# A one-core recommender tower: seventeen tables by one-hot, the Gram in 64x64 tiles ahead of the MLP, one-hots in halves

## The chip, the cores and the metric

The kernel runs on one core of one Trainium2 chip. The metric is the device time of one execution in microseconds (us); several runs of the same program are summed up by their median. The core has five engines with instruction queues of their own that meet only at semaphores: TensorE (PE, products; its weight loads are listed as PEld), VectorE (DVE), ScalarE (ACT), GpSimd (POOL) and SyncE (SP, which here only issues transfers).

## The reference

For each of 2048 samples, 32 categorical fields pick one row of 64 numbers each out of 32 tables. Of the tables 13 have 12500 rows, 2 have 125000, 8 have 1250 and 9 have 1000. The 32 rows of a sample are multiplied with each other (a 32x32 Gram matrix), the 496 entries above the diagonal and 16 dense inputs are the 512 inputs of a small network.

```python
e = jnp.stack([tbl_0[ids[:, 0]], ..., tbl_31[ids[:, 31]]], axis=1)    # 2048 x 32 x 64
gram = jnp.einsum('bnd,bmd->bnm', e, e)
z = gram[:, rows, cols]                                               # rows, cols: above the diagonal, 496
h = jnp.concatenate([z, dense_ctx], axis=1)                           # 2048 x 512
h = jnp.maximum(h @ W_top1 + b_top1, 0.0)                             # 512
h = jnp.maximum(h @ W_top2 + b_top2, 0.0)                             # 256
y = h @ W_top3                                                        # 2048 x 1
```

All of it is float32.

## The kernel before

**Supers and steps.** The batch is cut into 8 supers of 256 samples (two tiles of 128, `TILES`). Step `s` of the program turns super `s` into pairs of products, finishes the network of super `s - 1` and looks up rows of super `s + 1`. Steps 1 to 6 are a loop of three passes with two steps each; step 0 and step 7 stand outside it.

**Two ways to fetch a row.** The 16 smallest tables (`LOOKED_UP`, called units) are held in SBUF, each float32 split into three bfloat16 parts (`split_sb`). DVE compares the ids with the row numbers (`make_onehot`, L495) into a 0/1 tile `onehot` of 125 partitions x 8 or 10 columns x 256 samples, one instruction a unit; PE multiplies it with the parts (`look_up`, L303, 16 or 20 products a unit) and DVE adds the three parts into `rows` (`add_parts`, L503). A ring of four one-hots lets DVE run three units ahead. The other 16 fields are gathered by POOL: 32 indirect DMAs a super (L253), each followed by a write of zeros into a tile nobody reads (`pause`, L260), 256 of each in all. POOL does nothing else until the end, and it waits for no engine unless it comes two supers ahead.

**A step on PE.** Eight groups of four fields are transposed into `emb_t` (L289); from the second on, one unit of the next super goes before each. Groups 4 to 7 wait for the gathers. Then come eight Gram batches (L316) of 8 products each. A product takes four samples (64 rows x 128 columns, against 128 columns) and so holds the 32x32 blocks of each sample against all four, of which the four on the diagonal are wanted; samples of the first tile lie on partitions 0 to 63, those of the second on 64 to 127. The profile lists a float32 product as two records. Ahead of batches 0 to 4 stand two units each (one in the fifth), ahead of batches 4 and 5 the halves of layer 1 of the super before (L328), ahead of 6 layer 2 (L338), ahead of 7 layer 3 (L345).

**After a batch.** ACT copies one half of the Gram columns to `folded` (L441), then DVE lays the other half over it by a mask (L530); PE may start batch `k` once DVE is through with batch `k - 2`. When all eight are folded, 16 DMAs of 32 KB (L192) carry the wanted blocks from `folded` to `pairs`, and four more put the dense inputs beside them; ten of the 16 are issued by SP and six by POOL in the last step, all by SP before. ACT waits for them before the first copy of the next step, since there is one `folded`.

**Start and end.** Until the first transpose, PE, DVE and ACT split the tables and look up super 0. The last step has no units to look up: it transposes with four banks, and PE issues products on the identity (L352) to stay busy, 32 before the last group of gathers and 10 behind it.

The program as it stood, with the line numbers of the profile:

## Time and profile before

| what | value |
|---|---|
| runs, us | 494.22, 495.32, 491.78; median 494.22 |
| profiled execution, us | 495.87 |
| its span (first to last instruction), us | 493.6 |
| mean granted TensorE clock | 0.959 |
| busy us: PE, DVE, ACT, POOL | 432.1, 302.9, 114.2, 407.9 |
| instructions in the profile | 10400 |

Busy time is the time in which an engine had at least one instruction under way. Records of PE overlap, so that a mean duration of a record there is much longer than the distance from one to the next. What an engine waits for stands in brackets behind a row of the timeline; "issue" means that nothing in the profile released it at that moment. Lines such as L316 are lines of the kernel above.

### The profile page before, as it was taken

The numbers are of one execution on the slowest core, as the hardware profiler recorded it, in microseconds if no ns is written. First come the engines' busy times: TensorE is split into PE (matmuls) and PEld (weight loads), VectorE is DVE, ScalarE is ACT, GpSimd is POOL, SyncE is SP. The second block draws the span as 40 slices with busy tenths as digits, with TensorE's granted clock in tenths as the row PEclk, the third lists the DMA queues.
The fourth block names the chain that finished last, engine by engine and source line by source line (L and its number), as shares of the span: only waits on it lengthen the run. The fifth ranks groups of instructions, "written<-read, shape, count | busy, mean of one in ns | idle before, by whom it ended". The sixth has DMA issues, their size and how long they took to land.

```text
span 493.6 us, 10400 instructions
## 1 busy us (share of the span) xinstructions
PE 432.1 (88%) x4200; PEld 387.7 (79%) x4200; DVE 302.9 (61%) x369; ACT 114.2 (23%) x206; POOL 407.9 (83%) x522
## 2 busy tenths in 40 slices
PE   5298889989799989978999699988999679984987
PEld 5287789989598889877988599777988679874765
DVE  2499969968672698267925586366935847340400
ACT  2244313122012221231123110321113201230322
POOL 7999889999998899999988999889988999884110
PEclk9699999999999999999999899988999979995999
DMA  4534751012311222112311231122211231121010
GB/s 109 144 139 150 215 136 31 16 20 62 87 37 23 47 60 80 21 44 57 86 23 32 54 101 20 23 54 71 62 23 31 51 106 17 23 43 34 7 39 1
DMA packets 21814, 29.32 MB, mean 59 GB/s; under 512 B 9782, under 2 KB 14070, under 8 KB 20640
## 3 DMA queue, kind: packets, MB, share of 16 engines
q1 hardware_dynamic: 12980, 18.96, 11.3%
q0 software_dynamic: 8384, 8.60, 11.2%
q10 hardware_dynamic: 404, 1.09, 0.6%
q8 instruction: 37, 0.61, 0.5%
q14 instruction: 9, 0.07, 0.0%
HBM read 24.35 MB, written 0.07 MB: 49 GB/s over the span
## 4 chain that ended last, share of the span: by engine, by line
POOL 82%; issue 9%; PE 4%; DMA 2%; SPq 1%; DVE 1%; ACT 1%; DVEq 0%
POOL rows L253 59%; POOL pause L260 22%; PE mlp_ps L328 1%; PE gram_ps L316 1%; SPq L192 1%; PE mlp_ps L338 1%; DVE folded L530 1%; DMA rows<-tbl,index 0%; ACT folded L441 0%; PE gram_ps L352 0%; SPq L219 0%; DMA pairs<-dense 0%; DMA pairs<-folded 0%; DMA index<-ids 0%; PE turn_ps L289 0%
## 5 line engine op out<-in xcount | busy, mean ns | idle before, releaser
L253 POOL DMA_INDIRECT rows<-tbl,index x256 | 293.8, 1148 | 44.5 <-issue 42.1
L303 PE MATMUL turn_ps<-split_sb,onehot 125*128 125x192 bf16 x2272 | 213.5, 251 | 22.9 <-DVE split_sb L544 11.7
L303 PEld LDWEIGHTS turn_ps<-split_sb,onehot 125*128 125x128 bf16 x2272 | 193.7, 100 | 33.7 <-DVE split_sb L544 15.5
L495 DVE TENSOR_TENSOR onehot<-place,codes_wide 125x2048 bf16<-125x2048 f16 (+1 forms) x131 | 174.2, 1331 | 7.1 <-DMA place<-ids_scratch 7.1
L260 POOL MEMSET pause<- 128x384 f32 x256 | 111.5, 436 | 0.2
L503 DVE TENSOR_REDUCE rows<-turn_ps 128x128 f32<-128x384 f32 x128 | 71.1, 556 | 54.0 <-PE turn_ps L303 31.1
L530 DVE COPY_PREDICATED folded<-second_sb,gram_ps 128x512 f32<-128x512 int32 x64 | 46.7, 730 | 82.9 <-issue 47.7
L316 PE MATMUL gram_ps<-emb_t 64*128 64x128 f32 x1024 | 76.4, 288 | 3.7 <-DVE folded L530 2.2
L316 PEld LDWEIGHTS gram_ps<-emb_t 64*128 64x128 f32 x1024 | 63.8, 191 | 19.1 <-issue 14.8
L441 ACT COPY folded<-gram_ps 128x512 f32<-128x512 f32 x64 | 37.6, 587 | 150.4 <-PE gram_ps L316 132.3
L328 PE MATMUL mlp_ps<-pairs,w_sb 128*128 128x256 f32 x256 | 58.5, 383 | 1.2 <-DMA pairs<-dense 1.2
L404 ACT COPY emb_t<-mlp_ps 128x512 f32<-128x512 f32 x58 | 34.1, 588 | 101.2 <-PE mlp_ps L289 63.9
L289 PE MATMUL mlp_ps<-ident_sb,rows 128*128 128x128 f32 x240 | 38.8, 284 | 17.9 <-DMA rows<-tbl,index 11.3
L328 PEld LDWEIGHTS mlp_ps<-pairs,w_sb 128*128 128x128 f32 x256 | 47.5, 190 | 8.4 <-DMA pairs<-dense 1.7
L289 PEld LDWEIGHTS mlp_ps<-ident_sb,rows 128*128 128x128 f32 x240 | 27.5, 145 | 20.5 <-issue 19.0
L352 PE MATMUL gram_ps<-ident_sb 128*128 128x128 f32 x232 | 33.1, 301 | 4.5 <-DMA ident_sb<-identity 4.5
L352 PEld LDWEIGHTS gram_ps<-ident_sb 128*128 128x128 f32 x232 | 30.1, 158 | 4.5 <-DMA ident_sb<-identity 4.5
L338 PE MATMUL mlp_ps<-h,w_sb 128*128 128x256 f32 x128 | 29.6, 384 | 0.0
L421 ACT ACTIVATE h<-mlp_ps,b_sb 128x256 f32<-128x256 f32 x32 | 13.5, 472 | 58.7 <-PE mlp_ps L328 46.3
L338 PEld LDWEIGHTS mlp_ps<-h,w_sb 128*128 128x128 f32 x128 | 23.7, 190 | 3.8
L486 DVE COPY y<-mlp_ps 1x256 f32 (+1 forms) x8 | 5.0, 620 | 23.4 <-PE mlp_ps L345 23.4
L192 POOL DMA_DIRECT2D pairs<-folded x6 | 3.0, 513 | 17.6 <-DVE folded L530 17.6
(28 smaller groups left out, 75.7 us busy)
## 6 DMA issues: line engine op xcount, KB each, us to landing
place<-ids_scratch SPq DMA_DIRECT2D x8, 1000.0 KB
rows<-tbl,index POOLq DMA_INDIRECT x256
pairs<-folded SPq DMA_DIRECT2D x122, 32.0 KB
emb_t<-tbl SPq DMA_DIRECT2D x8, 250.0 KB
folded<-tbl SPq DMA_DIRECT2D x5, 312.5 KB
w_sb<-w SPq DMA_DIRECT2D x1, 1024.0 KB
place<-ids_scratch ACTq DMA_DIRECT2D x1, 750.0 KB
rows<-tbl SPq DMA_DIRECT2D x2, 312.5 KB
```

What stands on the lines that cost most here:

```text
L253: nc.gpsimd.indirect_dma_start(rows[:, s % 2, slot, t, :], None, tables[f][:, :], bass.IndirectOffsetOnAxis(index[:, s, t, f:f + 1], 0),). ...
L260: nc.gpsimd.memset(pause[:], 0.0).then_inc(paused, 1)
L289: last = nc.tensor.transpose(turn_bank[g % banks][:, k, :], rows[:, parity, GROUP_F * g + k].rearrange("p t d -> p (t d)"), ident_sb[:])
L303: last = nc.tensor.matmul(turn_ps[:, u % 2].rearrange("p k b -> p (k b)")[:, t * PARTS * DIM:(t + 1) * PARTS * DIM], onehot[:, u % RING, c ...
L316: last = nc.tensor.matmul(gram_ps[:, k % 2, t, u // TILES].rearrange("p h ij -> p (h ij)"), e.rearrange("p b f -> p (b f)"), e.rearrange(" ...
L328: last = nc.tensor.matmul(mlp_ps[:, o // 2, o % 2, :], w1_sb[:, jj, P * o:P * (o + 1)], pairs[:, parity, :, jj, :], start=(jj == 0), stop= ...
L338: last = nc.tensor.matmul(mlp_ps[:, 0, o, :], w2_sb[:, k, P * o:P * (o + 1)], h1[:, k, :], start=(k == 0), stop=(k == OT1 - 1))
L352: nc.tensor.transpose(gram_ps[:, 0, 0].rearrange("p u h ij -> p (u h ij)")[:, 0:P], ident_sb[:], ident_sb[:])
L441: nc.scalar.copy(folded[:, :, :, BATCH_Q * k:BATCH_Q * (k + 1)].rearrange("p i j (q t) -> p (i j) q t", t=TILES), gram_ps[:, k % 2, :, :, ...
L495: nc.vector.tensor_tensor(onehot[:, u % RING, 0:SPAN[u], :], place[:, parity, u, :].unsqueeze(1).to_broadcast([TP, SPAN[u], SUPER]), codes ...
L503: nc.vector.reduce_sum(rows[:, parity, u, :, :], turn_ps[:, u % 2].rearrange("p k b -> p (k b)")[:, 0:TILES * PARTS * DIM] .rearrange("p ( ...
L530: nc.vector.copy_predicated(folded[:, :, :, BATCH_Q * k:BATCH_Q * (k + 1)].rearrange("p i j (q t) -> p (i j) q t", t=TILES), second_sb[:]. ...
```

## The change

There are four edits.

1. `UNITS` goes from 16 to 17: the last table with 1250 rows is looked up as well, and POOL gathers 15 fields, 30 DMAs a super.
2. A Gram product takes two samples in place of four (64 rows x 64 columns, against 64 columns), and writes to partitions 0 to 63 or 64 to 127 of `gram_ps`. There are 128 products a super in place of 64, in four batches of 32, and a quarter of the columns each. `folded` has half the columns for a sample, two copies by parity, and ACT no longer waits for the moves.
3. The eight slots of the second half of a step remain, but only the first four have a Gram batch; the halves of layer 1, layer 2 and layer 3 stay ahead of slots 4 to 7.
4. `make_onehot` issues two instructions of half the columns.

PE in the loop's first step, from the fourth Gram batch on, before (`gram_ps` is the Gram's PSUM tile, `turn_ps` that of the units, `mlp_ps` that of the layers):

```order
L316 MATMUL gram_ps<-emb_t 128x128 [waits second_copied]
L316 MATMUL gram_ps<-emb_t 128x128 x7
L300 REGISTER_ALU [waits looked_up]
L303 MATMUL turn_ps<-split_sb,onehot 128x192 [waits onehot_ready]
L303 MATMUL turn_ps<-split_sb,onehot 128x192 x19
L324 REGISTER_ALU
L328 MATMUL mlp_ps<-pairs,w_sb 128x256 [waits dense_placed_even]
L328 MATMUL mlp_ps<-pairs,w_sb 128x256 x7
L311 REGISTER_ALU
L316 MATMUL gram_ps<-emb_t 128x128 [waits second_copied]
L316 MATMUL gram_ps<-emb_t 128x128 x7
L328 MATMUL mlp_ps<-pairs,w_sb 128x256 [waits y_ready]
```

And the same place now:

```order
L323 MATMUL gram_ps<-emb_t 64x64 [waits second_copied]
L323 MATMUL gram_ps<-emb_t 64x64 x31
L305 REGISTER_ALU [waits looked_up]
L308 MATMUL turn_ps<-split_sb,onehot 128x192 [waits onehot_ready]
L308 MATMUL turn_ps<-split_sb,onehot 128x192 x19
L305 REGISTER_ALU [waits looked_up]
L308 MATMUL turn_ps<-split_sb,onehot 128x192 [waits onehot_ready]
L308 MATMUL turn_ps<-split_sb,onehot 128x192 x19
L331 REGISTER_ALU
L335 MATMUL mlp_ps<-pairs,w_sb 128x256 [waits dense_placed_even]
L335 MATMUL mlp_ps<-pairs,w_sb 128x256 x7
L335 MATMUL mlp_ps<-pairs,w_sb 128x256 [waits y_ready]
```

The fourth batch is now the last, two units stand behind it in place of one, and the halves of layer 1 follow each other with no batch between them.

DVE in the same step, one Gram slot, before:

```order
L530 COPY_PREDICATED folded<-second_sb,gram_ps 128x64x8 [waits first_copied]
L502 REGISTER_ALU
L503 TENSOR_REDUCE rows<-turn_ps 128x128 [waits lookup_ready]
L495 TENSOR_TENSOR onehot<-place,codes_wide 125x2560
L502 REGISTER_ALU
L503 TENSOR_REDUCE rows<-turn_ps 128x128 [waits lookup_ready]
L495 TENSOR_TENSOR onehot<-place,codes_wide 125x2560
```

Now:

```order
L504 COPY_PREDICATED folded<-second_sb,gram_ps 128x32x16 [waits first_copied]
L525 REGISTER_ALU
L526 TENSOR_REDUCE rows<-turn_ps 128x128 [waits lookup_ready]
L518 TENSOR_TENSOR onehot<-place,codes_wide 125x1280 x2
L525 REGISTER_ALU
L526 TENSOR_REDUCE rows<-turn_ps 128x128 [waits lookup_ready]
L518 TENSOR_TENSOR onehot<-place,codes_wide 125x1280 x2
```

Each one-hot is two instructions now, and the fold has as many elements as before but of twice as many samples.

```diff
--- before.py
+++ after.py
...
-BATCH_Q = 8
+SIDE = 2
+SLOTS = 8
+BATCH_Q = 16
+GRAM_IN_SLOT = range(GRAM_BATCHES)
...
-LOOKED_UP = sorted(range(FIELDS), key=lambda f: (VOCAB[f], f))[:16]
+LOOKED_UP = sorted(range(FIELDS), key=lambda f: (VOCAB[f], f))[:17]
-FIRST_UNITS = 16
+FIRST_UNITS = 17
...
-GRAM_UNITS = [[7, 8], [9, 10], [11, 12], [13, 14], [15]]
+GRAM_UNITS = [[7, 8], [9, 10], [11, 12], [13, 14], [15, 16]]
-GRAM_UNITS += [[]] * (GRAM_BATCHES - len(GRAM_UNITS))
+GRAM_UNITS += [[]] * (SLOTS - len(GRAM_UNITS))
...
-    return rows, np.tile(second, (QUAD, QUAD))
+    return rows, np.tile(second, (QUAD, SIDE))
 def build(nc, ids, tables, dense, w1, b1, w2, b2, w3, identity, second, looked_ids, codes, out):
...
-        folded = sb("folded", [P, QUAD, HALF, QUADS], fp32)
+        folded = sb("folded", [P, 2, SIDE, HALF, QUADS], fp32)
...
-        second_sb = sb("second_sb", [P, QUAD * HALF], i32)
+        second_sb = sb("second_sb", [P, SIDE * HALF], i32)
...
-        spare = [(8, emb_t[0:TP].rearrange("p b f -> p (b f)")), (6, folded[0:TP].rearrange("p i j q -> p (i j q)")),
+        spare = [(8, emb_t[0:TP].rearrange("p b f -> p (b f)")), (6, folded[0:TP].rearrange("p h i j q -> p (h i j q)")),
...
-        gram_ps = ps("gram_ps", [P, 2, TILES, BATCH_Q // TILES, 2, QUAD * HALF], fp32)
+        gram_ps = ps("gram_ps", [P, 2, TILES, BATCH_Q // TILES, 2, SIDE * HALF], fp32)
...
         def move_cells(engine, i, jq, parity):
-                                    folded[FIELDS * i:FIELDS * (i + 1), i, CHUNKS * jq:CHUNKS * (jq + 1), :])
+                                    folded[FIELDS * i:FIELDS * (i + 1), parity, i % SIDE, CHUNKS * jq:CHUNKS * (jq + 1), :])
         def _(sp):
...
             def gram_batch(s, k):
-                for u in range(BATCH_Q):
-                    quad = BATCH_Q * k + u
-                    t, q = u % TILES, (BATCH_Q * k + u) // TILES
-                    e = emb_t[DIM * t:DIM * (t + 1), QUAD * q:QUAD * (q + 1), :]
-                    last = nc.tensor.matmul(gram_ps[:, k % 2, t, u // TILES].rearrange("p h ij -> p (h ij)"),
-                                            e.rearrange("p b f -> p (b f)"),
-                                            e.rearrange("p b (h j) -> p h b j", h=2),
-                                            start=True, stop=True)
+                for u in range(BATCH_Q // TILES):
+                    for i in range(0, QUAD, SIDE):
+                        for t in range(TILES):
+                            b = QUAD * (BATCH_Q // TILES * k + u) + i
+                            e = emb_t[DIM * t:DIM * (t + 1), b:b + SIDE, :]
+                            last = nc.tensor.matmul(
+                                gram_ps[FIELDS * i:FIELDS * (i + SIDE), k % 2, t, u].rearrange("p h ij -> p (h ij)"),
+                                e.rearrange("p b f -> p (b f)"), e.rearrange("p b (h j) -> p h b j", h=2),
+                                start=True, stop=True)
             def layer1_tile(s, o, parity, turn):
...
-                for k in range(GRAM_BATCHES):
+                for k in range(SLOTS):
...
-                    gram_batch(s, k)
+                    if k in GRAM_IN_SLOT:
+                        gram_batch(s, k)
...
+            def copy_first(s, k, parity):
+                act.wait_ge(gram_ready, GRAM_BATCHES * s + k + 1)
+                nc.scalar.copy(
+                    folded[:, parity, :, :, BATCH_Q * k:BATCH_Q * (k + 1)].rearrange("p i j (q t) -> p (i j) q t", t=TILES),
+                    gram_ps[:, k % 2, :, :, 0, :].rearrange("p t q ij -> p ij q t")).then_inc(first_copied, 1)
             def layer2_drain(s):
...
             def step(s, parity, mlp=True, ahead=True):
-                for k in range(GRAM_BATCHES):
+                for k in range(SLOTS):
-                    if k == 0 and (mlp or not ahead):
-                        act.wait_ge(pairs_moved, 16 * len(MOVES) * s)
-                    act.wait_ge(gram_ready, GRAM_BATCHES * s + k + 1)
-                    nc.scalar.copy(folded[:, :, :, BATCH_Q * k:BATCH_Q * (k + 1)].rearrange("p i j (q t) -> p (i j) q t", t=TILES),
-                                   gram_ps[:, k % 2, :, :, 0, :].rearrange("p t q ij -> p ij q t")).then_inc(first_copied, 1)
+                    if k in GRAM_IN_SLOT:
+                        copy_first(s, k, parity)
             def high(u):
...
+            def fold_second(s, k, parity):
+                dve.wait_ge(first_copied, GRAM_BATCHES * s + k + 1)
+                dve.sem_inc(folds_begun, 1)
+                nc.vector.copy_predicated(
+                    folded[:, parity, :, :, BATCH_Q * k:BATCH_Q * (k + 1)].rearrange("p i j (q t) -> p (i j) q t", t=TILES),
+                    second_sb[:].unsqueeze(2).unsqueeze(2).to_broadcast([P, SIDE * HALF, BATCH_Q // TILES, TILES]),
+                    gram_ps[:, k % 2, :, :, 1, :].rearrange("p t q ij -> p ij q t")).then_inc(second_copied, 1)
             def make_onehot(s, u, parity, first=False, loads=None):
-                nc.vector.tensor_tensor(onehot[:, u % RING, 0:SPAN[u], :],
-                                        place[:, parity, u, :].unsqueeze(1).to_broadcast([TP, SPAN[u], SUPER]),
-                                        codes_wide[:, CODE_AT[SPAN[u]]:CODE_AT[SPAN[u]] + SPAN[u], :],
-                                        ALU.is_equal).then_inc(onehot_ready, 1)
+                half = SPAN[u] // 2
+                for c in (0, half):
+                    code = CODE_AT[SPAN[u]] + c
+                    last = nc.vector.tensor_tensor(onehot[:, u % RING, c:c + half, :],
+                                                   place[:, parity, u, :].unsqueeze(1).to_broadcast([TP, half, SUPER]),
+                                                   codes_wide[:, code:code + half, :], ALU.is_equal)
+                last.then_inc(onehot_ready, 1)
             def add_parts(s, u, parity, first=False):
...
-                for k in range(GRAM_BATCHES):
+                for k in range(SLOTS):
-                        if k >= GRAM_BATCHES - READY_MADE:
-                            make_onehot(s + 2, k - (GRAM_BATCHES - READY_MADE), parity, loads=loads)
+                        if k >= SLOTS - READY_MADE:
+                            make_onehot(s + 2, k - (SLOTS - READY_MADE), parity, loads=loads)
-                    dve.wait_ge(first_copied, GRAM_BATCHES * s + k + 1)
-                    dve.sem_inc(folds_begun, 1)
-                    nc.vector.copy_predicated(
-                        folded[:, :, :, BATCH_Q * k:BATCH_Q * (k + 1)].rearrange("p i j (q t) -> p (i j) q t", t=TILES),
-                        second_sb[:].unsqueeze(2).unsqueeze(2).to_broadcast([P, QUAD * HALF, BATCH_Q // TILES, TILES]),
-                        gram_ps[:, k % 2, :, :, 1, :].rearrange("p t q ij -> p ij q t")).then_inc(second_copied, 1)
+                    if k in GRAM_IN_SLOT:
+                        fold_second(s, k, parity)
             def take_high(u):
```

The tables, ids and biases that the host lays out follow from `UNITS` and from `slot_meaning` by themselves.

## Rows read from the trace of the kernel before

**Rows 1.** The page, part 1: busy us of each engine, its share of the span, instructions.

```profile
PE 432.1 (88%) x4200; PEld 387.7 (79%) x4200; DVE 302.9 (61%) x369; ACT 114.2 (23%) x206; POOL 407.9 (83%) x522
```

**Rows 2.** The page, part 4: the chain that ended last, its shares of the span by line.

```profile
POOL rows L253 59%; POOL pause L260 22%; PE mlp_ps L328 1%; PE gram_ps L316 1%; SPq L192 1%; PE mlp_ps L338 1%; DVE folded L530 1%; DMA rows<-tbl,index 0%; ACT folded L441 0%; PE gram_ps L352 0%; SPq L219 0%; DMA pairs<-dense 0%; DMA pairs<-folded 0%; DMA index<-ids 0%; PE turn_ps L289 0%
```

**Rows 3.** Groups by form: line, engine, op, out<-in, shapes, count; busy us, mean ns; idle before.

```profile
L253 POOL DMA_INDIRECT rows<-tbl,index x256 | 293.8, 1148 | 44.5 <-issue 42.1 <-DMA index<-ids 2.4
...
L260 POOL MEMSET pause<- 128x384 f32 x256 | 111.5, 436 | 0.2
...
L495 DVE TENSOR_TENSOR onehot<-place,codes_wide 125x2048 bf16<-125x2048 f16 x75 | 91.0, 1215 | 7.1 <-DMA place<-ids_scratch 7.1
...
L495 DVE TENSOR_TENSOR onehot<-place,codes_wide 125x2560 bf16<-125x2560 f16 x56 | 83.3, 1487 | 0.0
...
L316 PE MATMUL gram_ps<-emb_t 64*128 64x128 f32 x1024 | 76.4, 288 | 3.7 <-DVE folded L530 2.2 <-issue 0.9 <-DVE rows L503 0.3
```

**Rows 4.** Instructions on tile rows, the gather alone: duration ns minimum/median/maximum.

```profile
L253 POOL DMA_INDIRECT rows<-tbl,index x256: 952/953/2427, 2.9 to 448.4; - x128
```

**Rows 5.** Timeline of POOL and DVE, 19 to 23 us: start us, duration us, engine, line.

```profile
19.27 1.23 DVE L495 TENSOR_TENSOR onehot<-place,codes_wide 125x2048 bf16<-125x2048 f16 x1 [7.13 <-DMA place<-ids_scratch]
...
20.09 1.23 POOL L253 DMA_INDIRECT rows<-tbl,index  x1 [0.17 <-issue]
...
20.41 0.68 DVE L539 TENSOR_TENSOR pairs<-emb_t,split_sb 125x512 f32<-125x512 f32 x1
...
21.61 1.22 DVE L495 TENSOR_TENSOR onehot<-place,codes_wide 125x2048 bf16<-125x2048 f16 x1
...
21.91 1.74 POOL L253 DMA_INDIRECT rows<-tbl,index  x1 [0.17 <-issue]
...
22.75 0.69 DVE L539 TENSOR_TENSOR h<-emb_t,split_sb 125x512 f32<-125x512 f32 x1
```

**Rows 6.** Timeline of PE while the small tables are split, to the first transpose.

```profile
60.12 1.81 PE L303 MATMUL turn_ps<-split_sb,onehot 125*128 125x192 bf16 x20 [0.43 <-issue]
...
63.46 1.81 PE L303 MATMUL turn_ps<-split_sb,onehot 125*128 125x192 bf16 x20 [0.43 <-issue]
...
71.41 0.66 PE L289 MATMUL mlp_ps<-ident_sb,rows 128*128 128x128 f32 x4 [0.65 <-DVE rows L503]
```

**Rows 7.** Timeline of PE, steps 0 to 4: first transposes, one Gram batch, one landing wait.

```profile
109.50 0.66 PE L289 MATMUL mlp_ps<-ident_sb,rows 128*128 128x128 f32 x4
...
184.92 1.16 PE L316 MATMUL gram_ps<-emb_t 64*128 64x128 f32 x16
...
186.02 3.47 PE L303 MATMUL turn_ps<-split_sb,onehot 125*128 125x192 bf16 x40
...
215.51 0.65 PE L289 MATMUL mlp_ps<-ident_sb,rows 128*128 128x128 f32 x4 [2.57 <-issue]
...
230.03 0.65 PE L289 MATMUL mlp_ps<-ident_sb,rows 128*128 128x128 f32 x4 [1.98 <-DMA rows<-tbl,index]
...
265.81 0.66 PE L289 MATMUL mlp_ps<-ident_sb,rows 128*128 128x128 f32 x4
```

**Rows 8.** Timeline of PE and POOL, the last step and the end.

```profile
435.47 0.66 PE L289 MATMUL mlp_ps<-ident_sb,rows 128*128 128x128 f32 x4
...
439.37 3.66 PE L352 MATMUL gram_ps<-ident_sb 128*128 128x128 f32 x32
...
448.39 0.95 POOL L253 DMA_INDIRECT rows<-tbl,index  x1 [0.17 <-issue]
...
450.89 1.11 PE L289 MATMUL turn_ps<-ident_sb,rows 128*128 128x128 f32 x4 [7.86 <-DMA rows<-tbl,index]
...
460.49 2.42 PE L316 MATMUL gram_ps<-emb_t 64*128 64x128 f32 x32 [0.30 <-DVE folded L530]
...
463.21 2.42 PE L316 MATMUL gram_ps<-emb_t 64*128 64x128 f32 x32 [0.30 <-DVE folded L530]
...
490.11 1.02 PE L345 MATMUL mlp_ps<-h,w_sb 128*1 128x256 f32 x4 [0.56 <-ACT h L427]
```

5 lines of the change are left out of this document (4 added, 1 removed).

## The prediction

> **What bounds the kernel now.** I read the chain of waits first. Four fifths of it are POOL: 59% gathers and 22% pauses [rows 2]. PE is busy for a larger share of the span, 88% [rows 1], so the second question is how much room PE has. It shows where the last group of transposes stands: PE waited 1.98 us for a landing in step 3 and 7.86 us in the last step [rows 7, 8]. POOL leads and PE follows a few per cent behind; both have to get shorter for the kernel to gain much.
>
> **POOL, its price list.** A gather takes 0.953 us when nothing meets it [rows 4] and 1.148 in the mean, the pause 0.436, and 42.1 us of issue over 256 is 0.164 [rows 3]. So a gather with its pause costs 1.553 bare, and on top come 293.8 - 256 x 0.953 = 49.8 us over the execution, 0.195 a gather. The early timeline shows what they are [rows 5]. The gather of 20.09 met the one-hot that ran from 19.27 to 20.50 and took 1.23; the one of 21.91 met the one-hot from 21.61 to 22.83 and took 1.74. Both agree with one rule: about 0.12 us after its start the gather needs something that the one-hot holds, and it gets it when that instruction ends (20.50 - 20.21 = 0.29 against 0.28 too long; 22.83 - 22.03 = 0.80 against 0.79). In both cases another instruction of DVE with two SBUF inputs had started 0.09 and 0.08 us before that end (20.41, 22.75), and the gather did not wait for this one too. So POOL gets through between two instructions that follow each other closely.
>
> The Trainium skill, "SBUF — State Buffer", section "Who interferes with whom", says the same: a DVE instruction with two SBUF inputs contends with a GpSimd instruction that reads SBUF, and the loser is blocked until the instruction ends. It would make nothing of the sum different.
>
> **Edit 4, halves.** One-hots cost 1.215 us for 2048 elements and 1.487 for 2560 [rows 3], so 0.531 ns an element and 0.127 fixed; a half is 0.671 or 0.807. What a gather that comes at a random moment waits is the sum of the squared durations over twice the period. Before: (9 x 1.215² + 7 x 1.487²)/2 = 14.4 over 32 x 1.748 = 55.9 us gives 0.258; measured are 0.195, or 0.76 of it, since the two engines are not independent. After: 9 x 0.671² + 8 x 0.807² = 9.3 over some 50.5 us gives 0.184, times 0.76 gives **0.14**. The ends: 0, and 0.22 if two halves hold POOL out like one instruction (0.195 x 17/16, over a period a tenth shorter). I take 0.14, since the rows at 20.41 and 22.75 are exactly this case.
>
> **Edit 1 on POOL.** 240 gathers in place of 256. The last one starts at 2.9 + 239 x (1.553 + 0.14) = 407.5; before it was 448.39 [rows 8]. That is 41 us earlier, of which 28 are the 16 gathers with their present price and 13 the shorter waits. Its rows land 2.5 later, at 410.
>
> **PE, its own pace.** First the start: the last units before the first transpose follow each other every 3.34 us (60.12 to 63.46) [rows 6], so a 17th unit costs that, and two instructions in place of one cost DVE 0.04 each time, as consecutive ones overlap by 0.09 and the fixed part is 0.127: 0.7 in all. Step 0 begins at 71.41 + 4.0 = 75.5.
>
> A step that waits for nothing takes 265.81 - 215.51 - 1.98 = 48.3 us, and the way back of the loop 2.57, once in two steps: 49.6 [rows 7]. Step 0 took 109.50 - 71.41 = 38.1, steps 1 and 2 together 215.51 - 109.50 = 106.0 [rows 6, 7]. A Gram batch costs 186.02 - 184.92 = 1.10, eight of them 8.8 a step. Unit 17 adds half of the 3.40 that 40 records of units take: 1.7 [rows 7]. Where no batch covers ACT, PE waits ahead of layer 3, 0.56 in the last row [rows 8]: 0.6 a step. So each of steps 1 to 6 loses 8.8 - 1.7 - 0.6 = 6.5, step 0 loses 7.1, and each gains G, the four new batches.
>
> **Edit 2, G.** The trace has no 64x64 tile; this is the term I know least. What it has: 16 records of 64x128 take 1.10 us, while a record's mean duration is 0.288 [rows 3, 7], so the two halves of the array do run side by side. A keep-warm product of the full array takes 3.66/32 = 0.114 [rows 8]. So a half takes as long for a record as the full array, and 16 in pairs take 8 x 0.112 = 0.9, plus 0.2 for draining at the change.
> - Low end: four tiles side by side, half the columns each. 64 records are 16 rounds of 0.056, with 0.2 behind: 1.1 a batch, G = 4.4.
> - Middle: only row halves overlap, column halves take turns: 32 rounds, 2.0 a batch, G = 8.0.
> - High end: a record costs 0.056 whatever its width, by its issue: 64 x 0.056 + 0.2 = 3.8, G = 15.1.
>
> I take 4.4, since the row halves overlap fully and two records of a pair cost no more than one.
>
> The Trainium skill, "TensorEngine Tiling (Array Packing)", section "Instruction Overhead", speaks against it: each matmul has some 60 cycles of overhead, so that a smaller one doesn't get cheaper. By its figure, an estimate of 25 ns for each of 64 records, a batch would be 1.8 us, G 7.2 and the time some 467. The trace shows no record that small.
>
> **The sum.** PE is through with step 6 at 75.5 + (38.1 - 7.1) + (106.0 + 4 x 49.6 - 6 x 6.5) + 7 G = 371.9 + 7 G, and stands ready for the last group 7.6 later (435.47 to 439.37 + 3.66) [rows 8]: 379.5 + 7 G, with G = 4.4 at **410.3**. POOL's rows are there at **410**. A tie, so each will at times wait for the other; I add 1.5 and let the last group start at 411.5, where it started at 450.89: 39.4 earlier.
>
> Behind it, two pairs of batches fall away, each 463.21 - 460.49 = 2.72 [rows 8], since a drain of the same size now serves 16 quads: 5.4 earlier. The moves, dense inputs and the two networks at the end stay. Span 493.6 - 39.4 - 5.4 = 448.8. The profiled execution was 2.3 longer than its span and 1.65 over the median of the runs, so I forecast 448.8 + 2.3 - 1.7 = **449.5**.
>
> **Costed at nothing**, with the cover named. DVE's work in a Gram slot, one fold, two sums and two one-hots, grows by 0.08 us; PE's slot was 1.1 + 3.4 us with no wait for DVE ahead of its batch [rows 7] and keeps that length. How much room DVE had there I can't read from these rows: if the halves bound it, three slots a step would grow by 0.1 each, 2 us in all. ACT's waiting for moves goes, but moves start four slots earlier now and layer 1 needs them a step later. `folded` at twice the copies moves the same bytes. The index of supers 1 to 7 is loaded behind 17 tables in place of 16, and POOL asks for it only at 2.9 + 30 x 1.7 = 54 us. The first three one-hots of the super after next are made in slots 5 to 7, while PE is in the layers. The layer-3 copy has one unit on PE to hide behind.
>
> **Rivals.**
> - *Column halves take turns* (chance 0.14). PE leads from G = 4.4 on. Before, the last batch ended at 463.21 + 2.42 = 465.6 [rows 8]; now it would end at the time at which PE is ready, plus 14 products of 0.114 (four transposes, ten to keep busy), plus G. With 8.0 that is 435.5 + 1.6 + 8.0 = 445.1, 20.5 earlier, or **474**. For it: no row shows a column tile. Against: the row halves.
> - *A floor per record* (0.10), whatever the tiles do: anything above 17 ns a record makes a batch longer than the 1.3 us at which PE clearly leads. At half the present 0.056 a batch is 2.0 us and the time again 474. For it: a quarter of the work in twice the instructions. Against: nothing in the present 0.056 needs one. The Trainium skill's page on tiling, cited above, is this rival's only source of a figure.
> - *Halves hold POOL out like a whole one-hot* (0.06). Then 0.22 a gather: the last start is at 2.9 + 239 x 1.773 = 426.6, 21.8 earlier, and with 5.4 behind it the time is **467**. Against it stand the rows at 20.41 and 22.75.
> - *PE's issue bounds and the kernel gets slower* (0.06). Twice the products, each at the old price of a record, in the Gram batches. The last batch ends at 379.5 + 7 G + 1.6 + G, which meets the 465.6 of before at G = 10.6, or (2.65 - 0.2)/64 = 38 ns a record. At the high end, 15.1, it ends at 501.9 and the time is **530**. Against it: two records and their loads now pass in 112 ns, and their width explains that.
> - *In between, G from 10 to 11* (0.03): within 1% of before.
> - *Fewer waits than I count* (0.04): with no waits of gathers POOL is done by 377, and PE sooner than my sum by some 4 us, as steps 1 and 2 (106.0 in place of 2 x 48.3 + 2.6) hold stalls that needn't come back: about 444.
>
> The rest, 0.57, is the forecast, from 443 to 458 by its bounds. The range takes in the first three rivals: 442 to 475. About 1% is what a measurement can tell from no change here. Faster by more than that 0.90, same 0.03, slower 0.07.
>
> **What would show it.** The gather's mean: 1.09 us if halves work, 1.17 if not. A Gram batch from its first product to the next unit: 1.1, 2.0 or 3.8 us for 64 records. The last group's wait for landed rows: near zero in a tie, some us if POOL still leads, none and a POOL that ends early if PE does; the chain of waits then is PE's. The start of the first transpose at 75.5. Gram batches at the end every 1.4 us. Wrong would be the whole reading if DVE's sums or one-hots released PE in the Gram slots.

## The result, and the profile after

| | before | after |
|---|---|---|
| median of the runs beside each other, us | 493.0 (4 runs) | 477.06 (475.72 to 479.38, 4 runs) |
| profiled execution, its span, us | 495.87, 493.6 | 479.38, 477.6 |
| granted clock | 0.959 | 0.939 |
| gathers: count, mean ns | 256, 1148 | 240, 1215 |
| start of the last gather, us | 448.39 | 437.38 |
| last group of transposes, us | 450.89 | 439.86 |

The ratio is 0.968 (95%: 0.962 to 0.974). The kernel got faster, but by 16 us and not by 44: the forecast was 449.5, the range ended at 475. Little more than a third of the expected gain arrived.

The chain of waits of the changed kernel, shares of the span by line, against [rows 2]:

```profile
POOL 83%; issue 9%; PE 4%; DMA 2%; SPq 2%; DVE 0%; ACT 0%; DVEq 0%
POOL rows L258 61%; POOL pause L265 22%; PE mlp_ps L335 2%; SPq L197 1%; PE gram_ps L323 1%; PE mlp_ps L345 1%; DMA rows<-tbl,index 1%; PE gram_ps L359 0%; DMA pairs<-dense 0%; SPq L224 0%; DMA pairs<-folded 0%; DMA index<-ids 0%; DVE folded L504 0%; ACT folded L434 0%; PE turn_ps L294 0%
```

POOL leads as before. The groups of POOL and of the Gram (line, engine, out<-in, count; busy us, mean ns; idle before), against [rows 3]:

```profile
L258 POOL DMA_INDIRECT rows<-tbl,index x240 | 291.6, 1215 | 41.8 <-issue 39.4
...
L265 POOL MEMSET pause<- 128x384 f32 x240 | 105.4, 439 | 0.1
...
L323 PE MATMUL gram_ps<-emb_t 64*64 64x64 f32 x2048 | 37.8, 223 | 0.7 <-DVE folded L504 0.7
```

Sixteen gathers fewer cost POOL almost as much busy time as before (293.8). The timeline of PE shows the rest: the first transpose, one batch, the first waits for rows, the way back of the loop, the last step and the end (start us, duration us):

```profile
75.34 0.66 PE L294 MATMUL mlp_ps<-ident_sb,rows 128*128 128x128 f32 x4 [0.65 <-DVE rows L526]
...
132.49 1.11 PE L294 MATMUL mlp_ps<-ident_sb,rows 128*128 128x128 f32 x4 [8.88 <-DMA rows<-tbl,index]
...
183.65 1.16 PE L323 MATMUL gram_ps<-emb_t 64*64 64x64 f32 x64
184.74 1.99 PE L308 MATMUL turn_ps<-split_sb,onehot 125*128 125x192 bf16 x22
...
217.30 0.68 PE L294 MATMUL mlp_ps<-ident_sb,rows 128*128 128x128 f32 x2 [3.62 <-issue]
222.51 0.58 PE L294 MATMUL mlp_ps<-ident_sb,rows 128*128 128x128 f32 x2 [4.52 <-issue]
...
424.74 0.66 PE L294 MATMUL mlp_ps<-ident_sb,rows 128*128 128x128 f32 x4
...
439.86 1.11 PE L294 MATMUL turn_ps<-ident_sb,rows 128*128 128x128 f32 x4 [7.89 <-DMA rows<-tbl,index]
...
474.06 1.02 PE L352 MATMUL mlp_ps<-h,w_sb 128*1 128x256 f32 x4 [0.56 <-ACT h L441]
```

The first transpose and the batch (184.74 - 183.65 = 1.09) are as forecast. What isn't: in step 1 PE waits 8.88 us for gathered rows, and in the last step 7.89.

**Where POOL's time went.** This is the start, POOL and then DVE:

```profile
43.80 0.43 POOL L265 MEMSET pause<- 128x384 f32 x1
44.39 2.81 POOL L258 DMA_INDIRECT rows<-tbl,index  x1 [0.17 <-issue]
47.20 0.43 POOL L265 MEMSET pause<- 128x384 f32 x1
```

```profile
43.36 1.55 DVE L518 TENSOR_TENSOR onehot<-place,codes_wide 125x1280 bf16<-125x1280 f16 x2
44.83 0.82 DVE L558 TENSOR_TENSOR h<-folded,split_sb 125x640 f32<-125x640 f32 x1
45.56 0.82 DVE L563 TENSOR_TENSOR split_sb<-pairs,split_sb 125x640 bf16<-125x640 f32 x1
46.30 0.55 DVE L526 TENSOR_REDUCE rows<-turn_ps 128x128 f32<-128x384 f32 x1
```

By the rule of [rows 5] the gather of 44.39 needs something at 44.51, meets the second half and gets it when that ends, at 44.91. It took 2.81 us; a free gather has 0.953 - 0.12 = 0.83 left from there, so it got it at 46.37, when the second subtraction ended (45.56 + 0.82 = 46.38). It was passed over at two boundaries between instructions with two SBUF inputs and got through only where the sum of parts, which reads PSUM, came next. The same in a Gram slot, and beside it a case that went well (gathers of POOL, then the one-hots on DVE that they met):

```profile
96.13 1.94 POOL L258 DMA_INDIRECT rows<-tbl,index  x1 [0.16 <-issue]
...
143.71 1.34 POOL L258 DMA_INDIRECT rows<-tbl,index  x1 [0.17 <-issue]
```

```profile
95.70 1.55 DVE L518 TENSOR_TENSOR onehot<-place,codes_wide 125x1280 bf16<-125x1280 f16 x2
...
143.41 1.55 DVE L518 TENSOR_TENSOR onehot<-place,codes_wide 125x1280 bf16<-125x1280 f16 x2
```

Each row is two halves of some 0.82, overlapping by 0.09. The gather of 143.71 got through at 143.71 + 1.34 - 0.83 = 144.22, the end of the first half (143.41 + 0.82). The one of 96.13 missed the end of the first (96.52) and got through at 97.24, the end of the second (97.25).

Counted over all gathers: above 240 x 0.953 they spend 63 us. 27 gathers were held past the end of the instruction that they met, 13 of them before the first transpose (17.1 us past it) and 14 later (10.2 us). These 27.3 us are nearly the whole distance from the forecast, which had 240 x 0.14 = 34 us of waits; without them the waits later are 0.139 a gather, where I had put 0.14. In the kernel before none was held so.

### The profile page after: what moved, and what is told of

It reads as the page before. It is cut to its first block, busy times and chain, and to the rows that moved or that the text cites. A ratio compares the mean times of both kernels' runs of the same rounds, so it can differ in the third digit from the quotient of the medians.

```text
span 477.6 us, 12826 instructions
## 1 busy us (share of the span) xinstructions
PE 407.4 (85%) x5394; PEld 373.2 (78%) x5394; DVE 307.2 (64%) x494; ACT 97.2 (20%) x176; POOL 399.6 (84%) x490
## 3 DMA queue, kind: packets, MB, share of 16 engines
q1 hardware_dynamic: 13110, 19.78, 12.4%
## 4 chain that ended last, share of the span: by engine, by line
POOL 83%; issue 9%; PE 4%; DMA 2%; SPq 2%; DVE 0%; ACT 0%; DVEq 0%
POOL rows L258 61%; POOL pause L265 22%; PE mlp_ps L335 2%; SPq L197 1%; PE gram_ps L323 1%; PE mlp_ps L345 1%; DMA rows<-tbl,index 1%; PE gram_ps L359 0%; DMA pairs<-dense 0%; SPq L224 0%; DMA pairs<-folded 0%; DMA index<-ids 0%; DVE folded L504 0%; ACT folded L434 0%; PE turn_ps L294 0%
## 5 line engine op out<-in xcount | busy, mean ns | idle before, releaser
L258 POOL DMA_INDIRECT rows<-tbl,index x240 | 291.6, 1215 | 41.8 <-issue 39.4
L308 PE MATMUL turn_ps<-split_sb,onehot 125*128 125x192 bf16 x2432 | 227.1, 252 | 18.9 <-DVE split_sb L563 16.2
L308 PEld LDWEIGHTS turn_ps<-split_sb,onehot 125*128 125x128 bf16 x2432 | 208.5, 100 | 26.5 <-DVE split_sb L563 20.8
L518 DVE TENSOR_TENSOR onehot<-place,codes_wide 125x1024 bf16<-125x1024 f16 (+1 forms) x278 | 194.4, 746 | 6.5 <-DMA place<-ids_scratch 6.5
L526 DVE TENSOR_REDUCE rows<-turn_ps 128x128 f32<-128x384 f32 x136 | 75.3, 554 | 56.9 <-PE turn_ps L308 53.2
L265 POOL MEMSET pause<- 128x384 f32 x240 | 105.4, 439 | 0.1
L434 ACT COPY folded<-gram_ps 128x512 f32<-128x512 f32 x32 | 18.8, 586 | 128.6 <-PE gram_ps L323 128.6
L323 PE MATMUL gram_ps<-emb_t 64*64 64x64 f32 x2048 | 37.8, 223 | 0.7 <-DVE folded L504 0.7
L323 PEld LDWEIGHTS gram_ps<-emb_t 64*64 64x64 f32 x2048 | 33.6, 137 | 5.7 <-issue 5.6
L504 DVE COPY_PREDICATED folded<-second_sb,gram_ps 128x512 f32<-128x512 int32 x32 | 23.1, 721 | 11.5 <-ACT folded L434 11.5
```

The costliest lines, as they stand in the source:

```text
L258: nc.gpsimd.indirect_dma_start(rows[:, s % 2, slot, t, :], None, tables[f][:, :], bass.IndirectOffsetOnAxis(index[:, s, t, f:f + 1], 0),). ...
L265: nc.gpsimd.memset(pause[:], 0.0).then_inc(paused, 1)
L308: last = nc.tensor.matmul(turn_ps[:, u % 2].rearrange("p k b -> p (k b)")[:, t * PARTS * DIM:(t + 1) * PARTS * DIM], onehot[:, u % RING, c ...
L323: last = nc.tensor.matmul(gram_ps[FIELDS * i:FIELDS * (i + SIDE), k % 2, t, u].rearrange("p h ij -> p (h ij)"), e.rearrange("p b f -> p (b ...
L504: nc.vector.copy_predicated(folded[:, parity, :, :, BATCH_Q * k:BATCH_Q * (k + 1)].rearrange("p i j (q t) -> p (i j) q t", t=TILES), secon ...
L518: last = nc.vector.tensor_tensor(onehot[:, u % RING, c:c + half, :], place[:, parity, u, :].unsqueeze(1).to_broadcast([TP, half, SUPER]), ...
```

## The experiments

The ratios are to the kernel before on the same chip; its median was 493.0, 493.2, 493.1, 492.9 and 491.0 in the five jobs (groups of kernels that ran beside each other). Jobs 1 and 2 ran on one chip, job 3 on a second, jobs 4 and 5 on a third. "Held" are gathers kept past the end of the instruction that they met. Where an expectation uses letters, A is the theory that POOL's losses at the boundaries are the cause, B that halves are innocent of them, L that PE's loop jump is the cause, F that the refill of `place` is, and S that the long Gram batches belong to one job and not to the kernel.

| run | job | median, us | ratio (95%) | waits of gathers beyond 0.953, us | held: count, us |
|---|---|---|---|---|---|
| the change | | 477.06 | 0.968 (0.962 to 0.974) | 63 | 27: 27.3 |
| e3 gaps | 1 | 478.16 | 0.967 (0.960 to 0.973) | 34 | 0 |
| f1 gaps again | 4 | 452.33 | 0.917 (0.914 to 0.921) | 36 | 0 |
| f4 change, refill early | 4 | 477.99 | 0.970 (0.965 to 0.976) | 61 | 25: 25.3 |
| e8 change, refill of one row | 2 | 478.13 | 0.969 (0.965 to 0.974) | 62 | 23: 23.8 |
| e11 whole one-hots, refill early | 3 | 470.41 | 0.956 (0.953 to 0.958) | 55 | 0 |
| f3 whole at the start alone | 4 | 466.36 | 0.944 (0.939 to 0.949) | 50 | 17: 12.4 |
| e4 before, halves | 1 | 496.74 | 1.007 (1.003 to 1.010) | 49 | 19: 20.8 |
| g2 before, halves | 5 | 498.96 | 1.013 (1.006 to 1.021) | 54 | 18: 20.0 |
| g1 before, halves, gaps | 5 | 479.35 | 0.975 (0.969 to 0.981) | 34 | 0 |
| e12 fastest | 3 | 442.45 | 0.900 (0.896 to 0.903) | 51 | 0 |

**Gaps (e3, f1, f2).** The direct test: a one-column memset of 0.06 us on DVE between the two halves, and around the subtractions of the start, so that no two instructions with two SBUF inputs follow each other directly in DVE's program. The work stays the same.

```diff
+            def gap_one():
+                n = next(gaps)
+                nc.vector.memset(gap[:, n:n + 1], 0.0)
...
                 for c in (0, half):
+                    if c:
+                        gap_one()
...
+                gap_one()
                 low(u)
+                gap_one()
```

> The change with a DVE write of one column (128x1, no SBUF input) between the two halves of each one-hot, and at the start also between the subtractions that follow, so that no two instructions with two SBUF inputs follow each other. Theory A: no gather waits past the end of the instruction it met; excess about 7 at the start and 0.14 x 209 = 29 us behind it, 36 in place of 63; PE then sets the end as often as POOL, time 450 to 456. Theory B: the excess stays near 63, time 477 or slightly more for the added instructions.

POOL did just this: none held, its last gather at 408.7. The time did not move: 478.16, and the chain was PE's. I took that for a second cause, the refill of `place`, and two more runs seemed to bear it out (below). But its profile had long Gram batches that nothing explained, so the same kernel ran again:

> The kernel with the one-column memset between two halves, run a second time, because its Gram batches need explaining: in its first profile 22 of its 28 batches of 64 records between units took 1.2 to 2.2 us where the changed kernel's take 1.09 to 1.14, 16.2 us in all, and they were long already in step 0, ahead of the first transfer of place that the other kernels treat differently. Theory F (the refill of place costs PE 27 us): about 478 again, with the long batches. Theory S (the long batches are something of that job and not of the kernel; the refill costs PE only what is left, 27 - 13 = 14 us over six steps): batches of 1.1 us and 478 - 16 = 462, with POOL's last gather near 410 as before.

The same kernel took 452.33, less than either theory had. This is one Gram batch of step 0 in the first run, and then in the second (PE's timeline):

```profile
92.38 1.14 PE L325 MATMUL gram_ps<-emb_t 64*64 64x64 f32 x58
93.83 0.36 PE L325 MATMUL gram_ps<-emb_t 64*64 64x64 f32 x6 [0.31 <-issue]
94.13 3.47 PE L310 MATMUL turn_ps<-split_sb,onehot 125*128 125x192 bf16 x40
```

```profile
91.97 1.16 PE L325 MATMUL gram_ps<-emb_t 64*64 64x64 f32 x64
93.06 3.47 PE L310 MATMUL turn_ps<-split_sb,onehot 125*128 125x192 bf16 x40
```

In job 1, PE stopped inside its batches with nothing to wait for; they took up to 2.4 us in place of 1.1 in all three kernels with the new Gram (9, 20 and 22 of the 28 batches between units in e1, e2 and e3), and in none of any other job. What it was I can't say. It isn't the chip, since job 2 had the same one, and the long batches are only 16 of the 29 us that PE lost in e3 against f1 between its first transpose and its last step. The kernel before ran at 493.0 in that job; old batches aren't free of it either, since e4 has two long ones of 28 and the profile of the kernel before has one. So of job 1 (e1 to e4) only POOL's counts carry weight here, and its times are given without resting on them. The second run's POOL, PE's rows in its last step, and the chain by engine:

```profile
L260 POOL DMA_INDIRECT rows<-tbl,index x240 | 264.4, 1101 | 41.9 <-issue 39.4 <-DMA index<-ids 2.6
```

```profile
403.47 0.66 PE L296 MATMUL mlp_ps<-ident_sb,rows 128*128 128x128 f32 x4
...
407.04 3.66 PE L361 MATMUL gram_ps<-ident_sb 128*128 128x128 f32 x32
412.99 0.66 PE L296 MATMUL turn_ps<-ident_sb,rows 128*128 128x128 f32 x4 [2.29 <-DMA rows<-tbl,index]
```

```profile
POOL 82%; issue 9%; PE 4%; DMA 2%; SPq 2%; DVE 0%; ACT 0%; DVEq 0%
```

A gather 1.10 us, PE ready at 407.04 + 3.66 = 410.7, the last group at 413.0, span 449.8: nearly every number of the forecast (1.09, 410.3, 411.5, 448.8). In DVE's rows the memset costs next to nothing:

```profile
43.41 1.56 DVE L526 TENSOR_TENSOR onehot<-place,codes_wide 125x1280 bf16<-125x1280 f16 x2
44.18 0.06 DVE L513 MEMSET gap<- 128x1 f32 x1
```

The two halves take 1.56 us together where they took 1.55, and their records still overlap, by some 0.07 us. So what lets a gather through is the instruction between them and no idle time of DVE that the profile would show.

Could the memset have helped only by moving the gathers away from the bad boundaries? The distances say no. In the change, each of the 14 gathers held in the steps needed the port 0.55 to 0.56 us after the start of a first half of 0.82 us, as the one of 96.13 did (96.13 + 0.12 - 95.70 = 0.55); none of the 37 that got through at a boundary did so there, and the one of 143.71 had 0.42. Over the seven kernels whose halves touch (the change, e2, e4, e8, f3, f4, g2), 80 gathers met a first half of 0.82 us at 0.54 to 0.58 us and 72 of them were held, while all that met a half in the steps at another distance, or a half of 0.68 us, got through at its end. In the seven with the memset between halves (e3, e5, e6, e7, f1, f2, g1) 75 gathers met such a half at the same distance, and none was held.

**The refill of `place` (e5, f2, e6, e8, e7, f4).** SP refills `place`, 1.06 MB, behind the moves. These now begin four slots earlier, so that a refill begins beside each of PE's two loop jumps (205.3 and 303.3 us in f1). e5 and f2 are the gap kernel with the refill ahead of the moves (`refill_place(2 * pair + 4, ...)` ahead of `rearrange_pairs(2 * pair + 1, 1)`, and so on); e6 and e8 shrink it to one row, with gaps and without, and so leave out the ids: from super 2 on they look rows up by old ones.

```diff
-                sp.dma_start(place[:, parity], scratch.ap()[bass.ds(of, 1)].to_broadcast([TP, UNITS, SUPER])
+                sp.dma_start(place[0:1, parity, 0:1], scratch.ap()[bass.ds(of, 1), 0:1]
```

> As e3_gap, and SP issues the refill of the ids' broadcast tile (place, 1.06 MB) for the super after next ahead of a super's moves in place of behind them. In e3_gap PE set the end: its loop-backs (steps 2 to 3 and 4 to 5) took 9 to 11 us from the last product to the second group of transposes, less 1.8 in a step without a jump, and each time a refill had begun within 1 us of the jump, and an instruction fetch took 2.9 us in place of 1.0. Theory F (the refill starves PE's instruction fetch): the jumps fall to about 3 us each, the last step begins 8 to 12 us earlier, time 466 to 470. Theory L (the jump is longer since the loop body holds more instructions): no change, 478 within 3.

> As e3_gap, but a refill of place carries one row of one partition in place of 1.06 MB, so that the supers from 2 on are looked up with ids of older ones; work, instructions and waits are otherwise the same. Theory F: jumps of about 3 us, stalls of PE inside the steps gone, the last group near the 412 us at which the rows have landed; time 450 to 456. Theory L: jumps as before, time 472 or more.

> The changed kernel itself with refills of one row (ids of supers from 2 on are old ones, otherwise the same work). In the changed kernel POOL ended last, PE waited 7.9 us for the last rows. So whatever the refill costs PE, the end stays with POOL: 474 to 478 under both theories, with jumps of about 3 us under F and a wait for the last rows of 20 us.

> The same kernel with the refill of place ahead of the moves, beside it in the same job. Both theories: 453, batches of 1.1 us. The difference to the run before is the price of the refill's place: 25 us by F, 9 by S.

> The changed kernel with nothing but the refill of place put ahead of the moves; halves follow each other without a gap. POOL's losses at the boundaries (27 us) are untouched, so by either theory POOL ends last, with its last gather near 437: 474 to 478. If the time falls clearly below 470, the losses come from the refill and not from the boundaries.

e5 452.95, e6 452.54, e8 478.13, f2 452.65, f4 477.99. Against e3's 478 the first two read like a gain of 25 us from moving one transfer. Against f1, 452.33 in the same job as f2, the gain is nothing (0.917 beside 0.919). With the gaps the refill can stay, come early or go: 452 to 453. Without them all three give 477 to 478. PE itself may feel it: its stops at the two jumps are 5.4 and 8.1 us in f1, where a refill runs beside both, and 5.7 and 5.8 in f2, where none does. POOL leads both kernels, so this doesn't reach the time. e7, which has gaps in the steps alone and whole one-hots at the start, with the early refill:

> Whole one-hots for super 0, halves with a one-column write between them behind it, refills ahead of the moves. Theory A and F together: POOL's excess 9 at the start and 27 behind it, first transpose at 74 in place of 76, jumps of about 3 us; PE 2 us ahead of e5_refill_early, time 464 to 468, the fastest of the kernels with full work so far. Under theory L about 475.

It took 453.56: how the start avoids the held gathers doesn't matter. Its expectation, and e5's, were too high because both counted on PE as it was in e3.

**Whole one-hots (e1, e11, e2, f3).** The fourth edit undone, for all supers or only before the first transpose.

```diff
-                half = SPAN[u] // 2
-                for c in (0, half):
+                half = SPAN[u]
+                for c in (0,):
```

> The change with edit 4 undone: each one-hot is one instruction again, the other three edits stay. Theory A (POOL often does not get in between two two-input DVE instructions that follow each other closely, and waits on to the end of the chain: 27 gathers of the changed kernel lose 27 us that way): the chains at the start are shorter again, so POOL's excess over 0.953 us a gather falls from 23.6 to about 7 us before the first transpose, and behind it rises from 39 to about 43 us, with no gather that waits past the end of the instruction it met. Sum 50 in place of 63: last gather 13 us earlier, time about 464. Theory B (the halves are innocent, the excess comes from 17 one-hots in a shorter step and from the phases of the two engines): whole one-hots have longer waits still, time 477 or more, up to 490.

> As e1_whole (edits 1 to 3, whole one-hots), with refills ahead of the moves. In e1_whole PE waited 8.3 us for the last rows, so POOL ends last and the refill's place is worth nothing there: 470 to 474. Beside e5_refill_early (453) this says what halves with a gap are worth once PE is free: 18 us. If the refill had delayed POOL itself, this would be 455 to 465.

> The change with whole one-hots for super 0 alone (while the tables are split), halves behind it. Theory A: excess at the start about 7 us in place of 23.6, behind it 39 as in the changed kernel; time about 461. Theory B: no difference to the changed kernel, 477 within 3.

> Whole one-hots for super 0 and halves after that, run a second time for the same reason (13.1 us of long batches in its first profile, last group ready at 432.7, POOL done at 415.8). F: 477. S: 477 - 13 = 464.

e1 took 472.54 and e11 470.41, with no gather held, but each pays for the longer one-hots: 0.238 and 0.233 us a gather after the start, more than e1's expectation had (57 us of waits in all, expected 50). Halves that follow each other closely are thus 7 to 8 us worse than whole one-hots (f4 beside e11), and halves with a gap 17 to 18 better (e5 beside e11); these pairs are from different jobs, in which the kernel before differs by 0.2 us. f3 took 466.36: the start is mended, 8.9 us of waits in place of 23.6, and in the steps 17 gathers are still held. e2, the same kernel in job 1, took 477.4, with runs from 470.3 to 480.3, and held 6. The difference in held gathers fits the distances above: 19 gathers of f3 met a first half of 0.82 us at the bad distance and 8 of e2, and two of each got through.

**Halves alone, on the kernel before (e4, g2, g1).**

```diff
-                nc.vector.tensor_tensor(onehot[:, u % RING, 0:SPAN[u], :],
...
+                half = SPAN[u] // 2
+                for c in (0, half):
...
+                    last = nc.vector.tensor_tensor(onehot[:, u % RING, c:c + half, :],
...
```

> The kernel before with edit 4 alone: each one-hot in two halves, nothing else. Theory A: excess at the start from 9 to about 23 us, behind it about the same 40 (shorter waits, but some that run on into the next half); 8 to 14 us slower than before, 501 to 507. Theory B: waits are halved and nothing is lost, excess 50 to 30 us, 473 to 480.

> The kernel before with halves that follow each other closely, a second time, beside the one with gaps, since its first run shared the job with kernels whose PE was slowed. POOL's waits were the same there as in the kernel before (48.6 against 49.8 us), so 492 to 495 if that job cost it anything, 497 again if not.

> The kernel before with the one-hot by halves and a one-column memset between two halves and between the subtractions of the start: the fourth edit alone, with the boundaries taken apart. If the boundaries are the whole reason why halves gain nothing, a gather's waits fall from 0.195 to 0.145 us as in the changed kernel with gaps, POOL's last gather starts 12 us earlier, at 436, and PE, ready at 443, becomes the bound: last group at 443 to 444 where it was 450.9, some 486 (0.985). If halves are of no use by themselves: 493.

e4 took 496.74 and g2 498.96, slower than before by 0.7% and 1.3%; with gaps (g1) 479.35. e4 was expected at 501 to 507. Its waits at the start grew as expected, to 21.6 us, but those in the steps fell to 27.0 from 40.8. The gather of g2 and then of g1:

```profile
L253 POOL DMA_INDIRECT rows<-tbl,index x256 | 297.7, 1163 | 44.5 <-issue 42.0 <-DMA index<-ids 2.6
```

```profile
L255 POOL DMA_INDIRECT rows<-tbl,index x256 | 277.6, 1084 | 44.4 <-issue 42.0 <-DMA index<-ids 2.4
```

20.1 us of gathers apart, 19.6 in time. g1 gained 7 us more than I expected of it: I had put PE ready at 443, from a step that held waits for rows, and it was ready at 429.8.

**The other edits alone (e9, e10).** e9 is the new Gram and its slots with 16 tables and whole one-hots, e10 the 17th table alone.

```diff
-LOOKED_UP = sorted(range(FIELDS), key=lambda f: (VOCAB[f], f))[:16]
-FIRST_UNITS = 16
-GRAM_UNITS = [[7, 8], [9, 10], [11, 12], [13, 14], [15]]
+LOOKED_UP = sorted(range(FIELDS), key=lambda f: (VOCAB[f], f))[:17]
+FIRST_UNITS = 17
+GRAM_UNITS = [[7, 8], [9, 10], [11, 12], [13, 14], [15, 16]]
```

> Edits 2 and 3 alone: 16 units, whole one-hots, Gram in 64x64 tiles in the first four slots. POOL has its 256 gathers and their waits, and it ends last, so PE's gain is hidden; only the end is shorter by the two pairs of batches, 5.4 us: 486 to 490. If PE had set the pace before, it would be 460 to 475.

> Edit 1 alone: 17 units, whole one-hots, the old Gram batches. POOL would be done by 433 as in e1_whole, but PE now has 1.7 us more a step and no relief: by the sum it is ready for the last group at 75.5 + 39.8 + 304.4 + 10.2 + 7.6 = 437.5; time 479 to 484. If only POOL counted, 476 or less.

e9 took 495.4 (1.007; 1.004 to 1.010), e10 481.02 (0.975; 0.972 to 0.978). A faster PE is worth nothing while POOL leads: in e9, expected at 486 to 490, PE waited 6.59 us for the last rows, and the gathers waited longer (1166 ns in the mean), so that the last group began at 455.27, 4.4 later than before, which took back most of what was saved behind it. In e10 PE has more to do and led; its last group had nothing to wait for:

```profile
430.94 3.66 PE L352 MATMUL gram_ps<-ident_sb 128*128 128x128 f32 x32
434.44 0.60 PE L289 MATMUL turn_ps<-ident_sb,rows 128*128 128x128 f32 x4
```

So the 17th table alone brings 12 us, the Gram alone nothing, halves alone cost about 1% (e4, g2). Together with gaps all four bring 41.

**The fastest (e12).** e7 with PE's loop written out and a pause of 256 columns in place of 384.

```diff
-PAUSE = 384
+PAUSE = 256
-            with pe.Fori(0, SUPERS // 2 - 1) as pair:
+            for pair in range(SUPERS // 2 - 1):
```

> As e7_whole_start_gap_early, PE's loop of steps 1 to 6 written out (no jump) and POOL's pause of 256 columns in place of 384. If the pause is only time, POOL is 0.14 us a gather faster and done by 380; PE loses two jumps of 6 to 7 us and its wait for the last rows: last group at about 396 in place of 412, time 435 to 440. If gathers need the pause (longer gathers in its place), POOL ends near 410 and the time stays 448 to 454.

It took 442.45. The pause fell from 439 to 328 ns, but gathers grew to 1167: of 27 us, 16 came back as waits (51 us in place of 35.5 in e7). PE's stops at the jump are gone. This is the step after the jump in f1, and the same in e12:

```profile
205.76 0.68 PE L296 MATMUL mlp_ps<-ident_sb,rows 128*128 128x128 f32 x2 [3.14 <-issue]
208.70 0.59 PE L296 MATMUL mlp_ps<-ident_sb,rows 128*128 128x128 f32 x2 [2.26 <-issue]
```

```profile
201.52 0.66 PE L300 MATMUL mlp_ps<-ident_sb,rows 128*128 128x128 f32 x4
202.02 1.16 PE L314 MATMUL turn_ps<-split_sb,onehot 125*128 125x192 bf16 x12
```

POOL still leads it: the last group waited 6.45 us for rows.

## Why the prediction failed

**What bounds the kernel: right.** POOL first, PE close behind it. The changed kernel is POOL's throughout, as [rows 2] had it.

**G, the new Gram batches: right.** 64 records take 1.09 us where [rows 7] had 16 in 1.10, G = 4.4. The single records of the batch at 183.65 start in sixteen groups of four, some 7 ns apart within a group and, after the first, 58 ns from group to group, where the old batch has pairs every 112 ns. So four tiles share the array in both directions, and that rival (474) and the floor per record (474) are out. The Trainium skill, "TensorEngine Tiling (Array Packing)", section "Instruction Overhead", gives some 60 cycles for each matmul, by the estimate in the prediction 25 ns for each of these records. Measured are 17 with the drain counted in, so taken for a record its figure does not hold here. Counted for a float32 product, two records, measured are 34 ns, and then nothing here speaks against the page.

**PE's own pace: right.** First transpose forecast at 75.5, measured 75.34; step 0 forecast at 35.4 and measured 35.0 (75.7 to 110.7 in f1). Steps 1 to 6 were to take 106.0 + 4 x 49.6 - 39 + 26.4 = 291.8; f1 has 403.47 - 110.7 = 292.8. They are made up otherwise than I thought: the stalls in the 106.0 of steps 1 and 2 didn't come back (95.1 from 110.7 to 205.8, where my terms give 101.8), and the jumps cost 5.4 and 8.1 us in place of 2.57. These errors cancelled. That the sum came out within 1 us is luck. A step without a jump takes 45.6 to 46.3, forecast 46.2.

**Behind the last group: right.** Forecast 5.4 shorter; [rows 8] give 493.6 - 450.89 = 42.7, the change 477.6 - 439.86 = 37.7.

**Edit 4: the step that failed.** "So POOL gets through between two instructions that follow each other closely" was read from the rows at 20.41 and 22.75 of [rows 5], two cases of one kind, both of a whole one-hot with a subtraction behind it. Then I took 0.14 for a gather's waits "since the rows at 20.41 and 22.75 are exactly this case", and bounded it at 0.22, a boundary that is never open. By its own words (0.195 x 17/16 over a period a tenth shorter) that bound is 0.23, and whole one-hots measured 0.229 over all gathers of e11. The change measured 63/240 = 0.262. Where gathers did get through, halving did what I worked out (0.139, and 0.148 over all of f1). But 27 did not. The bound itself was wrong too: without a gap a gather can be kept past the whole one-hot, to the end of a chain of four (2.81 us at 44.39), so the worst case was not one instruction of double length but the chain. The start, where halves and subtractions follow each other, took 17 of the 27 us. The kernel before has such boundaries as well, 36 of them, nearly all before the first transpose; 16 of its gathers came to one and all got through. Halving makes them 191 and puts one where every gather that meets a first half must pass it, and 64 gathers came to one. Nor do gathers come at random moments, as the sum of squares took them to: in the steps they were held up to three in a row, 4.48 us apart (from 96.13 on), each at the same place of its half. The waits without the held gathers came out at 0.14 all the same.

The Trainium skill, "SBUF — State Buffer", section "Who interferes with whom", calls the port pair an exclusive lock and says, of DVE's two-port modes, that who issues first has it for the whole instruction; the prediction read this as a block that ends with that instruction. In 27 cases here the gather was blocked longer; the page tells nothing of a second instruction right behind.

**Edit 1 on POOL: right but for that.** 240 gathers with these waits end at 437.4; without the 27 us held it is 410.5 in f1, forecast 407.5.

**Costed at nothing: held.** PE waited for DVE's folds 0.7 us in all, at the end. The refill, a transfer that moves with the moves and that I had not listed, cost the time nothing either (f1 beside f2).

**The rivals.** *Halves hold POOL out like a whole one-hot* (0.06, 467) was nearest in mechanism, but still too kind: halves are worse than that, by the 7 to 8 us between f4 and e11. No rival and no bound priced a gather that is passed over at a boundary, and the upper end of the range, 475, came from the Gram's rivals (474), which have no part in the 477.

**Open** is why a boundary stays shut. Of the change's gathers 37 got through at one and 27 did not. In the steps the distance and the length tell them apart, but for 8 of 80; at the start all 13 that were held met a second half with a subtraction behind it, 8 of them at 0.42 to 0.43 us of an 0.82 us half, where in the steps a first half let gathers through. No run shows what lies behind this. Open is also what slowed PE in job 1.

## What to carry to other kernels

Cutting a long instruction in two helps an engine that is waiting for its port reliably only if something that leaves the port alone stands between the pieces; here 0.06 us of memset turned a loss of 8 us (g2; 4 in e4) into a gain of 12 on the kernel before. When a rule rests on two rows of a profile, count it over all cases that the change will create, and let the upper bound be the whole chain and not one piece. And when a kernel's time contradicts its mechanism, run that same kernel again in another job before building a second cause on it: here this took away 25 us of "refill".

## What the runs showed of the hardware

- A gather that meets a DVE instruction with two SBUF inputs needs something about 0.12 us after its start, is held until that instruction ends, and has 0.83 us left. If a second such instruction follows closely, it passed in 37 cases of the change and was held on in 27, at most to the end of a chain of four. In the steps the held ones met a first half of 0.82 us at 0.54 to 0.58 us: 72 of 80 over seven kernels. With a memset of one column between the halves it passed every time, 75 of 75 at that distance in seven kernels.
- Products in 64x64 tiles on float32 run at 64 records in 1.09 us, drain included, four tiles at a time: four starts within 20 ns, the next four 58 ns later.
- The jump back of PE's loop cost 2.6 us in the kernel before [rows 7] and 5.4 to 8.1 in f1, in two stops with two records between them; written out (e12) PE has no stop there. A refill of 1.06 MB beside the jumps made no difference to the time; the stops sum to 13.5 us with it (f1) and 11.5 without (f2).
- One job ran the batches of 64 records and 64 weight loads, which take 1.1 us, with stops of 0.2 to 0.4 us in them (up to 2.4 us a batch; 478 us for the kernel), another without (452), and the kernel before took the same time in both.
